# Two score products in place of three: rounded Q and its rest stacked by DMA into the same 32 rows

## The reference

```python
q = heads(x @ Wq); k = heads(ctx @ Wk); v = heads(ctx @ Wv)   # 20 heads of 16
p = softmax(q @ k.T / sqrt(16))                               # 256 x 77 for each batch and head
x = merge(p @ v) @ Wo + bo + x                                # done twice, with the weights of layer 0 and 1
```

## Time and profile before

| | |
|---|---|
| median of 3 runs | 940.66 us (937.6 to 945.41) |
| the profiled execution | 941.04 us |
| its span in the trace | 939.2 us |
| PE busy | 903.8 us, 96% |
| DVE, ACT, POOL busy | 686.2, 544.1, 400.0 us |
| mean granted TensorE clock | 0.994 of full |

### The profile page before, as it was taken

The page is one execution under the profiler, slowest core; times in us unless marked ns, Lnnn a source line. Parts: engine busy times, 40 slices in busy tenths (PEclk is TensorE's granted clock), DMA queues, the critical chain, the costliest instruction groups (busy, mean ns, idle before and its releaser), DMA issues.

```text
span 939.2 us, 28086 instructions
## 1 busy us (share of the span) xinstructions
PE 903.8 (96%) x11518; PEld 685.7 (73%) x11518; DVE 686.2 (73%) x1223; ACT 544.1 (58%) x547; POOL 400.0 (43%) x227
## 2 busy tenths in 40 slices
PE   8899999999999999998999999999999999999797
PEld 5777778777777877776677687777778777777564
DVE  4776786867678686686768778786787878677456
ACT  4456565656666565565466656566565656656452
POOL 3433354624435453365443456354344625422223
PEclk9999999999999999999999999999999999999999
DMA  6313434544453544544455444444544544444342
GB/s 212 89 34 93 132 99 113 142 127 132 104 142 90 160 133 120 139 117 121 122 145 140 106 108 128 132 131 123 132 107 110 132 128 133 113 116 98 94 107 84
DMA packets 80526, 112.41 MB, mean 120 GB/s; under 512 B 21200, under 2 KB 37878, under 8 KB 80400
## 3 DMA queue, kind: packets, MB, share of 16 engines
q1 hardware_dynamic: 80400, 110.61, 44.3%
HBM read 60.24 MB, written 22.24 MB: 88 GB/s over the span
## 4 chain that ended last, share of the span: by engine, by line
PE 49%; DMA 17%; SPq 15%; DVE 8%; issue 6%; ACT 3%; POOL 1%; DVEq 0%; ACTq 0%; POOLq 0%
PE pR L306 18%; PE pR L432 8%; PE pA L379 6%; SPq L1389 6%; PE pR L366 5%; DMA X<-y 5%; DMA X<-in_xT 4%; DMA y<-X 4%; PE pR L286 2%; SPq L1359 2%; SPq L1396 2%; DMA out<-X 2%; PE pR L256 2%; SPq L1423 2%; ACT P L742 2%
## 5 line engine op out<-in xcount | busy, mean ns | idle before, releaser
L742 ACT ACTIVATE P<-pA 77x2048 f32<-77x2048 f32 x160 | 300.3, 1877 | 166.8 <-PE pA L385 166.6
L993 DVE TENSOR_REDUCE Mx<-pR 128x4 f32<-128x308 f32 (+1 forms) x480 | 258.9, 575 | 32.7 <-PE pR L366 27.5
L1252 POOL TENSOR_TENSOR On<-On,OS 128x1024 f32<-128x1024 f32 (+1 forms) x58 | 105.7, 1844 | 276.7 <-DMA OS<-rd 276.6
L306 PE MATMUL pR<-OS,Wo 128*128 128x512 f32 x638 | 170.1, 406 | 4.1 <-DVE OS L1049 3.3
L306 PE MATMUL pR<-XS,Wq 128*128 128x512 f32 x638 | 168.5, 403 | 2.7 <-POOL Wq L1238 1.6
L432 PE MATMUL pR<-P,VA 77*17 77x256 f32 x2480 | 156.8, 383 | 2.2 <-DVE Mx L993 1.6
L366 PEld LDWEIGHTS pR<-KH,QH 32*128 32x128 f32 x1280 | 96.5, 183 | 78.2 <-issue 43.7
L366 PE MATMUL pR<-KH,QH 32*128 32x154 f32 x1280 | 132.0, 284 | 15.4 <-ACT P L742 7.4
L379 PE MATMUL pA<-QH,KH 32*77 32x256 f32 x1280 | 145.6, 292 | 0.1
L306 PEld LDWEIGHTS pR<-OS,Wo 128*128 128x128 f32 x638 | 114.7, 189 | 34.6 <-issue 4.8
L306 PEld LDWEIGHTS pR<-XS,Wq 128*128 128x128 f32 x638 | 116.3, 189 | 31.8 <-POOL Wq L1238 2.0
(11 more groups left out here) (154 smaller groups left out, 1215.2 us busy)
## 6 DMA issues: line engine op xcount, KB each, us to landing
On<-Oraw SPq DMA_DIRECT2D x248, 64.0 KB, 2.7
OS<-rd SPq DMA_DIRECT2D x58, 256.0 KB
C<-in_cT SPq DMA_DIRECT2D x16, 616.0 KB, 8.0
X<-in_xT SPq DMA_DIRECT2D x16, 512.0 KB
y<-X SPq DMA_DIRECT2D x16, 512.0 KB, 4.2
X<-y SPq DMA_DIRECT2D x16, 512.0 KB
out<-X SPq DMA_DIRECT2D x15, 512.0 KB, 4.2
X<-in_xT SPq DMA_DIRECT2D x16, 256.0 KB
```

The costliest lines, as they stand in the source:

```text
L306: f = pe.matmul(p[:, :], W[:, k, c0:c0 + 128], S[:, s, :], start=(i == 0), stop=(i == len(pairs) - 1))
L742: act.activation(P[0:L, i % PR, :, :], pA[0:L, :, :], ACT.Exp, scale=float(D) ** -0.5).then_inc(p_done, 1)
L993: dve.tensor_reduce(Mx[:, :, :].rearrange("p t (j i) -> p j t i", j=4)[:, j:j + banks, :, i:i + 2], pR[:, bank:bank + banks, 0:2 * LK].rea ...
L1252: pool.tensor_tensor(On[rows, blocks, :], On[rows, blocks, :], recips(u, part).bitcast(F32), ALU.mult).then_inc(o_mul, 1)
```

## The change

The two heads of a pair no longer lie in 16 rows each but in alternate rows: the weights' columns are reordered on the host (`by_pair`), the mask is 1 in even or in odd rows. The rows of the other head, which in K are zero, are then used:

- `second_heads_out(n)` writes the odd rows of `QH` (rounded Q of the second heads) to DRAM, `qd`;
- `stack_first(n, part)`, when the row maxima of those blocks have been taken, copies the even rows of `QL` (rests of the first heads) into the odd rows of `QH`, and for each head p the rows of `KH` that hold K to the rows that hold zero;
- `stack_second(n, part)` reads `qd` into the even rows of `QL`, once the copy out of them has landed;
- `stack_keys(w)` moves the rests of K of the second heads from odd to even rows of `KL`.

Part 0 is block m=0, part 1 blocks 1 and 2. `QH` then holds rounded Q and rest of the first head, `QL` those of the second, and `KH` by either gives two of the three products at once: `keys_by_tokens` takes 4 steps and `run` 8. Four kinds of wait on these DMAs are added on PE ahead of `run(u, k)`. `KH` and `KL` hold all blocks in one tensor for two `w`. On ACT `split_x(u + 2)` goes behind `S(u, 1)` in even units, on PE the x-products of block m=2 wait for the rounded part first and the rest later, and the splits of `Wq` of layer 1 go ahead of those of x.

```diff
-        mask[(np.arange(128) // D) % 2 == p, p] = 1.0
+        mask[np.arange(128) % 2 == p, p] = 1.0
...
+def KAT(u, m, b):
+    return 5 * m + 2 * (u % 2) + b if m < 2 else 4 + 5 * (u % 2)
...
                 if m == 2:
+                    pe.wait_ge(x_hi, u + 1)
+                    for i, s in enumerate((0, 1, 3, 4, 2)):
+                        if s == 3:
+                            pe.wait_ge(x_lo, 2 * u + 1)
+                        if s == 2:
+                            pe.wait_ge(x_lo, 2 * u + 2)
+                        f = pe.matmul(p[:, :], Wq[:, s % 3, 256:384], XS[:, s, :], start=(i == 0), stop=(i == 4))
...
+                    if k == 0:
+                        pe.wait_ge(d_kl, 16 * (u // 2 + 1))
+                    if k in (0, 2):
+                        pe.wait_ge(d_qe[k // 2], 16 * (u + 1))
+                        pe.wait_ge(d_kf[k // 2], 32 * (u + 1))
+                    if k in (1, 3):
+                        pe.wait_ge(d_qb[k // 2], 16 * (u + 1))
...
-                    h = i // 3
+                    h = i // 2
-                    Q_ = (QH, QL, QH)[i % 3]
-                        kt = (KH, KH, KL)[i % 3][32 * j:32 * j + 32, ms, u % 4, h, :]
+                    kt = (KH, KL)[i % 2][32 * j:32 * j + 32, u // 2 % 2, KAT(u, ms, h), pp * L:pp * L + L]
+                    pe.matmul(pA[0:L, j, h * SQ:h * SQ + SQ], kt, (QH, QL)[pp][32 * j:32 * j + 32, u % 2, c0:c0 + SQ],
...
-                for step in range(10):
+                for step in range(8):
...
                         K(w, 1)
                         Q(u + 1, 1)
+                        if u == NCH - 2:
+                            weight_hi("Wq", 1)
+                        S(u, 1)
                         split_x(u + 2)
-                        S(u, 1)
...
+            def second_heads_out(n):
+                for m in range(3):
+                    sp.wait_ge(q_hi[m][n % 2], n // 2 + 1)
+                sp.dma_start(a["qd"][n], QH[1:128:2, n % 2, :].bitcast(F32)).then_inc(d_qo, 16)
+
+            def stack_first(n, part):
+                cols = slice(0, N) if part == 0 else slice(N, QC)
+                at0 = 2 * (n % 2) if part == 0 else 4 + 3 * (n % 2)
+                blocks = slice(at0, at0 + 2 + part)
+                for m in ((0,), (1, 2))[part]:
+                    sp.wait_ge(q_lo[m], n + 1)
+                    sp.wait_ge(k_lo[m], n // 2 + 1)
+                sp.wait_ge(x_pe, 2 * (NG * n + (2, 5)[part]))
+                sp.wait_ge(d_qo, 16 * (n + 1))
+                sp.dma_start(QH[1:128:2, n % 2, cols].bitcast(F32), QL[0:128:2, n % 2, cols].bitcast(F32)).then_inc(d_qe[part], 16)
+                for p in range(2):
+                    sp.dma_start(KH[1 - p:128:2, n // 2 % 2, blocks, p * L:p * L + L].bitcast(F32),
+                                 KH[p:128:2, n // 2 % 2, blocks, p * L:p * L + L].bitcast(F32)).then_inc(d_kf[part], 16)
+
+            def stack_second(n, part):
+                cols = slice(0, N) if part == 0 else slice(N, QC)
+                sp.wait_ge(d_qe[part], 16 * (n + 1))
+                sp.dma_start(QL[0:128:2, n % 2, cols].bitcast(F32), a["qd"][n][:, cols]).then_inc(d_qb[part], 16)
+
+            def stack_keys(w):
+                for m in range(3):
+                    sp.wait_ge(k_lo[m], w + 1)
+                sp.dma_start(KL[0:128:2, w % 2, :, L:2 * L].bitcast(F32), KL[1:128:2, w % 2, :, L:2 * L].bitcast(F32)).then_inc(d_kl, 16)
...
             weight_load("Wo", 0)
+            second_heads_out(0)
+            stack_keys(0)
+            stack_first(0, 0)
+            stack_second(0, 0)
             values(0)
+            stack_first(0, 1)
+            stack_second(0, 1)
...
                     put_recips(v, 1)
+                    second_heads_out(n)
                     spread(v, 0)
                     spread(v, 1)
+                    stack_first(n, 0)
                     store(z)
+                    stack_second(n, 0)
                     load_c(u // 2 + 2)
                     sums(u, 0)
+                    stack_first(n, 1)
                     load_x(u + 3)
+                    stack_second(n, 1)
                 else:
...
+                    second_heads_out(n)
                     values(u + 1)
                     spread(v, 0)
                     spread(v, 1)
+                    stack_first(n, 0)
                     store(z)
+                    stack_second(n, 0)
+                    stack_keys(u // 2 + 1)
                     sums(u, 0)
+                    stack_first(n, 1)
+                    stack_second(n, 1)
```

More of the change, by code:

```diff
@@ L141, in build @@
         d_zt, d_rwt, d_rbt, d_ont = (sem(f"d_{n}") for n in ("zt", "rwt", "rbt", "ont"))
+        d_qo = sem("d_qo")
+        d_qe, d_qb, d_kf = ([sem(f"d_{n}{i}") for i in range(2)] for n in ("qe", "qb", "kf"))
+        d_kl = sem("d_kl")
         d_w = {n: sem(f"d_{n}") for n in ("Wk", "Wv", "Wq", "Wo")}
@@ L394, in run @@
                             f = tokens_by_keys(step, j)
-                        if 2 <= step < 8 and u is not None:
+                        if 2 <= step < 6 and u is not None:
                             keys_by_tokens(step - 2, j)
-                        if step >= 8 and u is not None:
-                            g = less_maxima(step - 8, j)
+                        if step >= 6 and u is not None:
+                            g = less_maxima(step - 6, j)
                     if n is not None and step == 1:
                         f.then_inc(x_pe, 1)
-                    if u is not None and step == 9:
+                    if u is not None and step == 7:
                         g.then_inc(s_pe, 1)
-                    if n is not None and step == 8:
+                    if n is not None and step == 6:
                         take_pair(second, 1)
                     for j in (2, 3):
-                        if step < 6 and u is not None:
+                        if step < 4 and u is not None:
                             keys_by_tokens(step, j)
[L409 to L413, removed]
+                        if 4 <= step < 6 and u is not None:
+                            less_maxima(step - 4, j)
+                        if step >= 6 and n is not None:
+                            f = tokens_by_keys(step - 6, j)
+                    if n is not None and step == 7:
                         f.then_inc(x_pe, 1)
@@ L652, in K @@
                     if m < 2:
-                        f = act.activation(KH[:, m, first:first + 2, :, p * L:p * L + L].rearrange("p s b k -> p (s b) k"),
+                        f = act.activation(KH[:, w % 2, 5 * m:5 * m + 4, p * L:p * L + L],
                                            psum(slot["K", w, m])[:, 0:L4].rearrange("p (b k) -> p b k", k=L),
@@ L656, in K @@
                     else:
-                        f = act.activation(KH2[:, first:first + 2, p * L:p * L + L],
+                        f = act.activation(KH[:, w % 2, 4:10:5, p * L:p * L + L],
                                            Kt[:, :].rearrange("p (s b k) -> p s b k", s=2, b=2)[:, :, 0, :],
@@ L1277, in _ @@
                     split_o(u - 2)
-                    split_x(u + 2)
                     if u == NCH - 2:
                         weight_lo("Wq", 1)
+                    split_x(u + 2)
                     normalise(u - 1, 0)
@@ L1566 @@
     aps["rd"] = nc.dram_tensor("rd", (NU, H * N), F32, kind="Internal").ap()
+    aps["qd"] = nc.dram_tensor("qd", (NU, 64, QC), F32, kind="Internal").ap()
     aps["out"] = nc.dram_tensor("out_0", (C, TOK), F32, kind="ExternalOutput").ap()
```

48 lines of the change are left out of this document (22 added, 26 removed).

## The result

The changed kernel took 1064.78 us (median of 4 runs, 1060.45 to 1067.39), the kernel before 942.62 beside it: ratio 1.1298, 95% interval 1.1232 to 1.1364. The forecast was 995 within 925 to 1035. The direction was right and the loss more than twice as large: 122 us in place of 54. The profiled execution has a span of 1061.9 us, against 939.2.

The account below looks back on a forecast made before the run. PE bounds the kernel before; after the change SP's queue and PE's wait for keys were to set 59.2 us a pair. 941.0 + 14 x (59.2 - 55.8) + 6 = 994.6, said as 995 us, range 925 to 1035.

Parts of the forecast that it names:

- The products: Score runs on PE: 10 steps become 8, nothing hidden, saving 0.227 us in each of 160 runs, 36.3 us.
- Rival E: The two products on PE run slower than a step each, runs keep 1.39 us, SP still pays: near 1000; chance 0.05.
- SP's round: SP's queue as a closed round, waiting only for its own DMAs: 38.5 + 12.4 + 7.2 + 1.0, 59.1 us a pair.
- Issues on SP: 19 added DMA issues a pair in SP's queue at 0.65 us each: 12.4 us; bounds 7.6 and 16.
- Waits of `stack_second`: SP waits for the first copy of `stack_first` to land, twice a unit: 7.2 us a pair; bounds 1 and 12.
- The wait of 1.65 us for the reciprocals to reach DRAM: SP's idle gap in even units, read as waiting for reciprocals; one issue of 0.65 fills part, 1.0 us stays.
- The wait for keys: PE at `run(u, 0)` of even units stalls for the copy by `stack_keys`: 4.4 us, a pair of 57.3.
- The clock: After PE's stall on keys the granted clock is lower: 0.29 x 5 us, 1.5 us lost, giving 58.8 a pair.
- The start: `values(0)` and `load_x(2)` stand behind unit 0's stacks, S(0, 1) comes later: 6 us counted; bounds 2 and 10.
- The end: The last three units save 3 x 1.15 us and meet one more stall on keys: 0 in sum.
- rival D: DMA side: more bytes and 308-byte pieces lengthen every landing, 62 to 65 us a pair, 1030 to 1075; chance 0.10.
- The rule of the Trainium skill: Issue time on a queue is usually small beside the DMA itself; by it the 19 issues would cost nothing.

Follow-up runs that it names:

- e1: Changed kernel with all DMAs of the stacks and the waits on them left out: 926.98 us, ratio 0.9829 to the kernel before.
- e2: Changed kernel with the reciprocals of the sums later in DVE's order: 1038.55 us, ratio 1.1008 to the kernel before.
- e3: Changed kernel with `stack_keys` issued ahead, in the even unit before: 1073.5 us, ratio 1.14 to the kernel before.
- i2: Changed kernel with `stack_first(n, 0)` ahead of `spread` on SP in both kinds of unit: 1068.92 us, ratio 1.1313 to the kernel before.
- g1: Changed kernel, all 19 issues a pair kept but 64 columns each, `stack_second` without its wait and into other columns: 998.68 us, ratio 1.0588.
- f2: Changed kernel with the DMAs of the stacks issued from POOL's queue, same bytes: 1084.52 us, ratio 1.149 to the kernel before.
- f3: Kernel before with 19 more DMAs of 1 KB a pair to DRAM on SP, waited for only at the end: 1130.1 us, ratio 1.1975.

## Why the prediction failed, step by step

*The products* (36.3 us saved): wrong. The step that failed is "nothing of these steps is hidden, they stand in PE's own order". They do, but a run also waits for a bank within it, and e1 saves 16 us. Rival E had part of this, for another reason. The 995 doesn't rest on this step, since SP's round sets it and the saving is not a term of that.

*Issues on SP* (19 x 0.65 = 12.4 a pair): right. From one issue to the next, gaps under 0.2 us included, SP spent 527.3 us on 771 issues before and 708.1 on 1035 after in the 14 pairs, 37.7 and 50.6 a pair: 12.9 more, at 0.68 each. My base of 38.5, taken from one pair, was 0.8 too high. The issues of the K copies lasted 0.68 on average, no more than the others.

*Waits of `stack_second`* (7.2 a pair): 71.5 / 14 = 5.1. The places were right: `QH<-QL` of part 0 landed 5.4 us after its issue, where `spread` stands ahead, that of part 1 after 2.5.

*"The wait of 1.65 us for the reciprocals to reach DRAM"*: misread. SP waits there for PE's `out(z, 2)`, as the view of waits of the kernel before says (29.6 us in 14); its five matmuls ran from 613.04 to 614.44, and the issue went out at 614.52. I kept the wait at 1.0 a pair; it became 66.7 / 14 = 4.8.

*SP's round, 59.1 a pair*: this is the step on which the forecast fell, with its reason, "SP waits in it only for its own DMAs". By the timeline a pair is 50.6 of issues, 5.1 for the copies, 4.8 for PE ahead of `spread`, and 2.0 for sums, splits, maxima products and small gaps: 62.5. Against my 59.1 the issues are 0.3 less and the copies 2.1 less; the other waits are 6.8, 5.8 more than the 1.0 that I gave them. SP's round is not closed: it also waits for other engines, for PE's `out` above all, and in the pair shown these in turn waited for what SP had issued late. The moves bear out that this is a loop, though no run opens it: what one removed (PE on `X` in e2, on `KL` in e3, SP on PE in i2) came back at other places, and the times stayed between 1038 and 1079.

*The wait for keys* (4.4 us a pair): 33.5 us in 15, 2.2 each. In the pair shown the keys were issued 26.8 us after PE's first run of unit 19 (649.29), where I had some 23.4; but PE too got to the next run only after 28.0, not 22.1, and stood 2.06.

*The clock* (1.5 us a pair, 21 in all): more. PE busy came to 934.3 us, where I had 868 plus slow phases. PE has the same instructions in e1 and in the changed kernel and is busy 889.0 against 934.3 us. So 45 of the 140 us between them are slower matmuls behind stalls, and 94 are idle time.

*The start* (6): 12.4. `load_x(2)` went out at 46.02 as forecast (45), but ACT had its split at 55.78 and S(0, 1) at 57.79, and unit 0, from its `max_rows` on, took 40.0 us in place of 31.0.

*The end* (0): 12.8, in units 29 and 30 and the tail, for which I had counted nothing. The missing sum, then: 14 x the pair's error of 3.6 us is some 50 of the 69 us, start and end 19.

The time is the one of rival D (1030 to 1075, chance 0.10), but its reason, longer landings by bytes, is not the largest part: g1 with thin copies loses 72 us, the bytes 26 to 41. *The rule of the Trainium skill* ("DMA: Bandwidth & Descriptors", section "Issuing engines are not separate DMA queues") would have made the issues nearly free; here they take 12.9 us more of SP in a pair, and g1, which has little but them, loses 72 us. The page has it that issuing from other engines only saves such time; in f2 it saved SP's, and the time was 1084.5, since the waits moved to POOL with the issues.

What stays open: by which share g1's 72 us come from SP's longer round and which from later sums. A second buffer for `OS`, which would take PE out of `spread`, was not tried.

## What to carry to other kernels

A DMA queue that also serves the other engines is part of their loop: price an added issue or wait by walking the loop once round (who waits for what stands behind, and does that come back), not by adding up the queue. Read each wait of the queue from the view of waits before giving it a reason. And a saving inside an engine's busy time counts only down to the next thing that this time was covering, such as another engine's read of a bank.

## What was not expected of the hardware

19 DMAs a pair of 128 pieces of 8 bytes to DRAM, waited for only at the kernel's end, cost 187 us (f3), more than twice what 19 thin copies did (72), though both are 19 issues; why is open. And one stall is dearer than its length: behind 3.93 us of waiting the granted clock was 0.69 in the next 5 us, and the 94 us of idle time that PE has more than in e1 go with 45 us of slower matmuls.
